# One-token shift of x1 made by two SBUF-to-SBUF transfers instead of three matmuls and a copy

## The reference, cut to what matters

```python
def shift_token(t):
    t1, t2 = jnp.split(t, 2, axis=-1)
    t2 = jnp.pad(t2, ((0, 0), (1, 0), (0, 0)))[:, :-1]
    return jnp.concatenate([t1, t2], axis=-1)
...
x = x + o @ wo                       # x1
h = shift_token(x)                   # the shift in question
mu = h.mean(-1, keepdims=True)
var = h.var(-1, keepdims=True)
h = (h - mu) / jnp.sqrt(var + 1e-05) * lg + lb
h = h @ w1 + b1
a, g = jnp.split(h, 2, axis=-1)
x = x + (a * jax.nn.gelu(g, approximate=False)) @ w2 + b2
```

## Time and profile before

| | |
|---|---|
| median of 3 runs | 1540.19 us (1538.37 to 1541.11) |
| the profiled execution | 1538.19 us |
| its span, first to last instruction | 1536.4 us |
| TensorE matmul busy | 1456.6 us, 95% |
| VectorE busy | 1132.7 us, 74% |
| ScalarE busy | 939.0 us, 61% |
| GpSimd busy | 746.6 us, 49% |
| mean granted TensorE clock | 0.983 of full speed |

### The profile page before, as it was taken

One profiled execution on the slowest core, in us unless ns is written; L12 is line 12 of the kernel. 1 busy time (PEld: TensorE's weight loads), 2 busy tenths in 40 slices (PEclk: granted clock), 3 DMA queues, 4 the chain that ended last, 5 costly groups with the idle time before them and its releaser, 6 DMA issues.

```text
span 1536.4 us, 33772 instructions
## 1 busy us (share of the span) xinstructions
PE 1456.6 (95%) x11936; PEld 1292.5 (84%) x11936; DVE 1132.7 (74%) x3102; ACT 939.0 (61%) x2670; POOL 746.6 (49%) x571
## 2 busy tenths in 40 slices
PE   4999999868999999999999899999999999999997
PEld 3888888746888899988888788888888888888887
DVE  3766666456787788777778778878878787878874
ACT  2766666435666666666666566666666666666662
POOL 1111211145666666565555555555555555555652
PEclk9999999889999999999999999999999999999999
DMA  6211111200000000000000100101000000000000
GB/s 195 102 61 44 51 59 36 90 21 22 22 22 22 22 22 20 20 20 22 26 21 22 53 28 22 29 28 29 29 29 29 27 27 27 27 27 28 28 29 22
DMA packets 37148, 56.05 MB, mean 36 GB/s; under 512 B 5616, under 2 KB 18752, under 8 KB 37056
## 3 DMA queue, kind: packets, MB, share of 16 engines
q1 hardware_dynamic: 37056, 54.85, 11.2%
HBM read 38.06 MB, written 16.78 MB: 36 GB/s over the span
## 4 chain that ended last, share of the span: by engine, by line
PE 77%; DVE 12%; issue 4%; ACT 4%; SPq 1%; DMA 1%; POOL 1%; DVEq 0%; ACTq 0%; POOLq 0%
PE pb L486 33%; PE pb L756 9%; PE pb L708 6%; PE pb L770 6%; PE pb L739 5%; PE pb L723 4%; PE pb L794 4%; PE pb L547 2%; PE pb L535 2%; PE pb L585 2%; PE pb L589 2%; DVE p_t L1353 2%; DVE r_cos L1318 2%; DVE n_sq L1304 1%; DVE p_t L1339 1%
## 5 line engine op out<-in xcount | busy, mean ns | idle before, releaser
L1530 POOL TENSOR_TENSOR n_inv<-n_cl,half_neg 128x16 f32<-128x16 f32 x64 | 211.1, 3298 | 205.7 <-DVE n_cl L1309 202.2
L1026 ACT ACTIVATE p_t<-p_t,s_nm 128x128 f32<-128x128 f32 (+1 forms) x512 | 226.7, 446 | 34.2 <-DVE s_nm L1339 33.6
L486 PE MATMUL pb<-h_hi,w_hi 128*128 128x256 f32 x704 | 208.3, 296 | 6.0 <-DVE h_lo L1300 3.3
L486 PE MATMUL pb<-h_lo,w_hi 128*128 128x256 f32 x704 | 199.3, 283 | 0.0
L486 PE MATMUL pb<-h_hi,w_lo 128*128 128x256 f32 x704 | 199.2, 283 | 0.0
L1535 POOL TENSOR_TENSOR r_cos<-r_cos,r_sin 128x1024 f32<-128x1024 f32 x64 | 154.6, 2415 | 87.8 <-DVE r_sin L1324 87.8
L984 ACT ACTIVATE qk_sq<-pb 128x512 f32<-128x512 f32 x128 | 72.4, 591 | 183.2 <-PE pb L486 183.2
L1339 DVE CUSTOM_DVE_ANT_0 p_t<-pb,mask_t 128x128 f32<-128x128 f32 (+1 forms) x512 | 152.0, 354 | 43.0 <-PE pb L708 27.2
L1017 ACT ACTIVATE pt_t<-pb 128x512 f32<-128x512 f32 x192 | 114.3, 596 | 106.5 <-PE pb L723 105.6
L486 PE MATMUL pb<-wqkv_hi,xt_hi 128*128 128x512 f32 x384 | 166.7, 434 | 5.8 <-DVE r_sin L1324 4.9
L1557 POOL TENSOR_TENSOR hg_lo<-hg,hg_hi 128x256 fp32r<-128x256 f32 x192 | 139.4, 746 | 54.8 <-DVE hg_hi L1370 54.8
(11 more groups left out here) (138 smaller groups left out, 4151.9 us busy)
## 6 DMA issues: line engine op xcount, KB each, us to landing
x_cur<-y_state SPq DMA_DIRECT2D x32, 256.0 KB, 2.6
x_res<-y_state SPq DMA_DIRECT2D x32, 256.0 KB, 2.6
x_in<-x SPq DMA_DIRECT2D x16, 256.0 KB, 2.9
x_state<-x_x SPq DMA_DIRECT2D x16, 256.0 KB, 2.1
y_state<-y_x SPq DMA_DIRECT2D x16, 256.0 KB, 2.1
y_state<-x SPq DMA_DIRECT2D x16, 256.0 KB, 2.1
x_orig<-x_state SPq DMA_DIRECT2D x16, 256.0 KB, 2.8
out<-x SPq DMA_DIRECT2D x16, 256.0 KB, 2.2
```

The lines of the kernel that those rows point to most:

```text
L486: mm = pe.matmul(dst, s, m, start=(n == 0 and k == 0), stop=(n == len(pairs) - 1 and k == 2))
L1026: e = nc.scalar.activation(pu, pu, ACT.Exp, bias=s_nm[:, j, k:k + 1], scale=-1.0, accum_out=s_sum[:, j, k:k + 1])
L1530: nc.gpsimd.tensor_tensor(n_inv[:, t], n_cl[:, t], half_neg[:], ALU.pow).then_inc(pool_inv, 1)
```

## The change

shift_down moves from TensorE to SyncE and copy_shifted goes away. Two DMAs copy slot 2 to slot 1 inside x1, one partition further: 127 rows of both tiles in the first, and the one row that crosses from tile 0 to tile 1 in the second. Row 0 of tile 0 stays zero from a memset on GpSimd made once ahead of the layers, for which SyncE waits at g = 2. stats_h waits for both transfers (32 counts of a new semaphore, shift_load), weigh(b,0) waits for dve_x1. In SyncE's list the x_cur load moves from the head of an iteration to its end. The identity input shrinks from 260 to 128 columns.

```diff
-def identities():
-
-    return np.eye(P, 2 * P + 4, k=4, dtype=np.float32)
+def identity():
+    return np.eye(P, dtype=np.float32)
...
-        ones_at = sb("ones_at", [P, 2 * P + 4])
-        id_f, down_f, carry_f = ones_at[:, 4:4 + P], ones_at[:, 3:3 + P], ones_at[:, 3 + P:3 + 2 * P]
+        ones_at = sb("ones_at", [P, P])
+        id_f = ones_at[:]
...
+            def shift_down(c):
+
+                sp.dma_start(x1[1:P, :, 1], x1[0:P - 1, :, 2]).then_inc(shift_load, 16)
+                sp.dma_start(x1[0:1, 1, 1], x1[P - 1:P, 0, 2]).then_inc(shift_load, 16)
+
             def run_l(g, layer=None):
                 a, b, c, d, par = l_roles(g)
-                if has_next(a):
-                    sp.wait_ge(pe_xt, at(a, 1, 1))
-                    sp.dma_start(x_cur[:], one(y_dram, seq_of(plus(a, 1), layer))).then_inc(cur_load, 16)
+                if isinstance(g, int) and g == 2:
+                    sp.wait_ge(zero_made, 2)
                 if c is not None:
                     sp.wait_ge(dve_x1, at(c, 1, 1))
+                    shift_down(c)
                     if b is not None:
                         sp.dma_start(x_res[:], one(y_dram, seq_of(b, layer))).then_inc(res_load, 16)
...
                         sp.dma_start(x_orig[:], one(x1_dram, seq_of(c, layer))).then_inc(orig_load, 16)
+                if has_next(a):
+                    sp.wait_ge(pe_xt, at(a, 1, 1))
+                    sp.dma_start(x_cur[:], one(y_dram, seq_of(plus(a, 1), layer))).then_inc(cur_load, 16)
...
-            def shift_down(c):
-
-                pe.wait_ge(dve_x1, at(c, 1, 1))
-                pe.matmul(pb[:, 6, 0:P], down_f, x1[:, 0, 2], start=True, stop=True)
-                pe.matmul(pb[:, 6, P:2 * P], down_f, x1[:, 1, 2], start=True, stop=False)
-                pe.matmul(pb[:, 6, P:2 * P], carry_f, x1[:, 0, 2], start=False, stop=True).then_inc(pe_down, 1)
...
-                        pe.wait_ge(dve_down, at(c, 1, 1))
+                        pe.wait_ge(dve_x1, at(c, 1, 1))
...
-            def copy_shifted(c):
-                dve.wait_ge(pe_down, at(c, 1, 1))
-                nc.vector.tensor_copy(x1[:, :, 1], pb[:, 6, 0:2 * P].rearrange("p (t n) -> p t n", t=NT)).then_inc(dve_down, 1)
-
             def stats_h(c):
-                dve.wait_ge(dve_down, at(c, 1, 1))
+                dve.wait_ge(shift_load, at(c, 32, 32))
...
+            nc.gpsimd.memset(x1[:, 0, 1], 0.0)
             nc.gpsimd.memset(hg_hi[:, FC - 1].bitcast(F32), 0.0)
```

More of the change, by code:

```diff
@@ L253, in build @@
             "cur_load", "res_load", "orig_load", "x2_store")]
-        pe_down, dve_down = sem("pe_down"), sem("dve_down")
+        shift_load = sem("shift_load")
         pe_xt, act_xhi, dve_xlo = sem("pe_xt"), sem("act_xhi"), sem("dve_xlo")
@@ L803, in run_l @@
                     project(a, d, 0, 1)
-                if c is not None:
-                    shift_down(c)
                 if a is not None:
@@ L1398, in run_l @@
                 if c is not None:
-                    copy_shifted(c)
                     stats_h(c)
@@ L1617 @@
         "w2": rows_padded(L0_ffn_w2, FC * P), "b2": np.asarray(L0_ffn_b2),
-        "rope": rope_tables(), "mask": masks(), "ident": identities(),
+        "rope": rope_tables(), "mask": masks(), "ident": identity(),
     }
```

## The result

The changed kernel takes 1825.49 us (median of 4 runs, 1823.73 to 1826.46) against 1539.9 us (4 runs): a ratio of 1.1855, 95% interval 1.1841 to 1.187. It is slower by 285.6 us. The forecast was 1793 us, with a range of 1690 to 1890. The profiled execution took 1826.46 us, its span is 1824.6 us.

What follows compares the result with a forecast made beforehand. TensorE, busy 1456.6 of 1536.4 us, was taken as the bound. Rotation stalls net of removal 108, last iterations 10, x_cur 62 and clock 73 make 253 us on 1538.19, 1791; plus 2.0 to the median, 1793 us, range 1690 to 1890.

Steps and rivals of the forecast that it cites:

- Removed, 21 us: TensorE loses three shift matmuls per iteration: 0.67 us saved each time, 21 us over 32 iterations.
- One engine: The 127-row shift copy puts all 254 packets on one DMA engine; main case, 82%.
- the rule in the prediction: A DMA uses as many engines as the largest divisor, up to 16, of its partitions: 77 gives 11, 127 gives 1.
- The landing, 8.3 us: Shift copy from issue to landing: 0.9 us to first data, 7.0 us of packets, 0.4 us behind the last.
- The formula of the Trainium skill: Cost of a GpSimd-issued DMA, 2.0 us plus bytes over 436 GB/s; at a sixteenth of the rate, 6.8 us.
- Stall before the rotation's projection: TensorE waits 4.3 us before project(1,0), net +3.6 us after the removal; 108 us over thirty iterations.
- The last two iterations: No projection there, so the statistics themselves are waited for: 5 us each, 10 us.
- x_cur: Late load stalls TensorE before turn_next: +1.5 us per iteration in layer 0, +3.1 in layer 1, together 62 us.
- The clock, 60 us of the 73: TensorE's clock falls to 1.2 GHz after stalls: 2.0 us for 30 stalls, 60 us; layer 1's x_cur stalls, 13 us.
- the spread copy: Rival: the big copy is spread over 16 engines, no rotation stall, x_cur still late; 1594 us, 10%.
- The faster rival: The copy is spread and x_cur comes in time, so only the removal is left: 1519 us, 3%.

Runs made afterwards that it cites:

- experiment 1: Changed kernel with x_cur load first: 1758.49 us; with copy cut into 112 + 15 rows: 1594.23; with both: 1524.31. Kernel before with only x_cur load moved last: 1611.14.
- experiment 2: Changed kernel with the x_cur load first and the 127-row copy cut into 126 + 1 rows: 1524.44 us.
- The filler: Changed kernel with 18 matmuls, whose result nothing reads, ahead of TensorE's wait for the rotation in project(1,0): 1757.44 us.
- experiment 3: Changed kernel with its two shift copies in the other order, the one-row copy first: 1827.25 us.
- experiment 5: Changed kernel with x_cur load first and stats_h later in VectorE's list: 1644.31 us; with add_parts also ahead of deviation in GpSimd's list: 1568.04 us.

## Why the prediction was right, and where its sizes were off

- **Removed, 21 us.** The steady iterations gained 0.6 to 0.7 us against 0.67 forecast; in all it came to 15.7 and 15.1 us (experiments 1 and 2), where 2 to 3 us more went into waits for the rotation.
- **One engine.** Right, and decisive: 231 us by experiment 1, 234 by experiment 2. The reading that carried it was the count of small packets, 43 = 16 + 16 + 11; the changed kernel's count has a single completion for its 127 rows, as the rule in the prediction had it.
- **The landing, 8.3 us: the term that was too small.** It was 9.5 us. The packets were nearly right, 28.5 ns each where I had drawn 27 ns from a line between two traffic rows of other sizes; that is 0.2 of the 1.2 us. The rest is what stands around the data, which I took from a 128-partition store to DRAM: 1.4 us to the first data instead of 0.9, and 0.8 us behind the last instead of 0.4. The formula of the Trainium skill, which the prediction quotes beside its sum (DMA: Bandwidth & Descriptors; it stands in the section "Anatomy of one DMA — SWDGE (gpsimd) path"), gave an estimate of 6.8 us; the measured 9.5 us differ from it and decide.
- **Stall before the rotation's projection.** Forecast 4.3 us gross, measured 5.0 on the mean of 30: it follows the landing, as VectorE's work behind it took 3.5 us where 3.7 were forecast. The last two iterations took 9.3 and 6.6 us, not 5 each.
- **x_cur.** 62 us forecast, 63.9 us of waits measured, and 67.0, 69.9 and 71.2 us by taking the edit out or putting it in. The clock's 13 us on top were too many: 3 to 9 us remain for that.
- **The clock, 60 us of the 73.** Forecast 2.0 us for each of 30 stalls, measured 2.0 on the mean in the stretch behind it. The filler gave back 68 us.
- **From 1793 to 1825.** Summed up, the sizes that were off give 21 us (30 stalls, 0.7 us longer each), 6 us (the last two iterations), 5 us (the removal) and 8 us (the clock by the filler), less 4 to 8 us (x_cur with its clock): 32 to 36 us, and the measured time is 32 us over the forecast.
- **Do the parts add?** The one-engine copy costs 231 us with x_cur late and 234 with x_cur early, and x_cur costs 67 to 71 us in three settings, so the two add within 4 us. With the removal, 231 + 70 - 16 is 285 us, but these three differences add up to the measured one in any case, as each starts from the kernel at which the next ends.

Of the rivals, the spread copy named its own price well: 1594 us, and the kernel that spreads the copy and leaves x_cur late ran in 1594.23. That it hit to the microsecond is partly luck: the removal gave 5 us less than its 21, and x_cur with its clock cost 5 us less than its 75. The faster rival, 1519 us, is what the kernel with both repairs comes near, 1524 us.

## What to carry to other kernels

Before a compute step is replaced by a DMA, count the partitions it moves: 127 rows ran on one DMA engine and 126 on fourteen, and here the load of 77 partitions showed the rule in its completion packets before anything was built. Then find what the waiting engine has queued behind that wait, and where in its own queue a moved load now stands: here both stood ahead of TensorE, and each stall of 5 us was paid again with 2 us of clock. Of the kernels run here, the shift by transfer beat the kernel before only with both mended, 1524 against 1540 us.

## What the runs showed of the hardware that I had not expected

- SyncE itself is held when one DMA engine has many packets before it: the DMA issued behind the 254 packets took 4.8 us to issue, a copy of 512 B (940.89) and a load of 256 KB (942.12 in experiment 3) alike. When the same 254 packets were spread, the issues behind them took 0.5 to 0.9 us. The hold ends before the engine is done: the issue was over at 945.80, the copy's data at 948.75. All that stands behind it in SyncE's list is late too. Here nothing there was urgent.
- A contiguous row of 512 B was cut into 16 parts of 32 B with 16 completions, while 127 rows of 512 B were not spread at all.
- VectorE's norm (TENSOR_SCALAR, SBUF to SBUF) took up to 2,495 ns instead of 408 beside a GpSimd add of 2.4 us, which was not slowed. Taking the two apart was worth 76 us over the run (experiment 5). The Trainium skill (SBUF — State Buffer, "Who interferes with whom") says that such an instruction can take a pair of ports that VectorE shares with GpSimd, and that whoever issues first has it for its whole instruction, with the other blocked. The trace agrees, with the norm's first instruction starting 0.06 us after the add and lasting until it ended; the ports themselves no trace shows.
